# A recommender tower on one core: the last tile's second bias added on TensorE, its results stored as a column

## The reference

```
e = jnp.stack([tbl_0[ids[:, 0]], ..., tbl_31[ids[:, 31]]], axis=1)   # [2048, 32, 256]
dots = jnp.einsum('bnd,bmd->bnm', e, e)
z = dots[:, iu, ju]                                                  # i < j: 496 numbers
h = jnp.concatenate([z, dense_ctx], axis=1)                          # [2048, 512]
h = jnp.maximum(h @ W_top1 + b_top1, 0.0)                            # 512 -> 512
h = jnp.maximum(h @ W_top2 + b_top2, 0.0)                            # 512 -> 256
y = h @ W_top3                                                       # 256 -> 1
```

## Time and profile before

| | |
|---|---|
| median of 3 timed runs | 561.64 us (561.14 to 562.19) |
| the profiled execution: its own time | 563.57 us |
| its span, first to last instruction | 561.7 us |
| mean granted clock of TensorE | 0.988 of full speed |
| TensorE products, busy | 508.8 us, 91% of the span |
| VectorE, ScalarE, GpSimd busy | 45%, 33%, 71% |

### The profile page before, as it was taken

One profiled execution on the slowest core, in us unless ns is written; L12 is line 12 of the kernel. 1 busy time (PEld: TensorE's weight loads), 2 busy tenths in 40 slices (PEclk: granted clock), 3 DMA queues, 4 the chain that ended last, 5 costly groups with the idle time before them and its releaser, 6 DMA issues.

```text
span 561.7 us, 24241 instructions
## 1 busy us (share of the span) xinstructions
PE 508.8 (91%) x11019; PEld 467.3 (83%) x11019; DVE 250.8 (45%) x593; ACT 183.6 (33%) x354; POOL 397.6 (71%) x426
## 2 busy tenths in 40 slices
PE   0775799999899989999999999989998999989986
PEld 0765699999799979999989988979987899979885
DVE  3666362734336362343636263354626335351421
ACT  1786060513206051230505151140505114050422
POOL 6777577777777777777777777777777777777600
PEclk9997999999999999999999999999999999999998
DMA  8999344444444444444444444444444444433300
GB/s 190 272 261 305 116 117 125 118 120 116 124 121 125 118 116 118 121 125 116 124 121 120 124 113 119 121 125 117 117 128 113 122 116 118 116 107 106 97 2 1
DMA packets 37459, 70.97 MB, mean 126 GB/s; under 512 B 10382, under 2 KB 23438, under 8 KB 37358
## 3 DMA queue, kind: packets, MB, share of 16 engines
q0 software_dynamic: 20112, 54.95, 35.0%
q1 hardware_dynamic: 17246, 14.48, 10.4%
HBM read 69.39 MB, written 0.01 MB: 124 GB/s over the span
## 4 chain that ended last, share of the span: by engine, by line
PE 77%; DMA 7%; POOL 5%; issue 5%; ACT 3%; DVE 2%; DVEq 0%; ACTq 0%; POOLq 0%
PE look_ps L342 31%; PE quad_ps L364 16%; PE top_ps L415 10%; DMA rows<-in_tbl,row_ids 7%; PE turn_ps L326 6%; PE quad_ps L326 6%; POOL rows L299 5%; PE top_ps L428 5%; PE quad_ps L385 1%; PE top_ps L405 1%; DVE small L688 1%; DVE turned L626 1%; ACT area L526 1%; ACT products L520 0%; ACT turned L496 0%
## 5 line engine op out<-in xcount | busy, mean ns | idle before, releaser
L299 POOL DMA_INDIRECT rows<-in_tbl,row_ids x419 | 396.8, 947 | 132.1 <-issue 116.1
L342 PE MATMUL look_ps<-one_hot,small 125*128 125x256 f32 (+1 forms) x1536 | 221.0, 293 | 8.3 <-DVE small L688 8.0
L342 PEld LDWEIGHTS look_ps<-one_hot,small 125*128 125x128 f32 x1536 | 195.1, 192 | 11.9 <-issue 9.3
L698 DVE TENSOR_SCALAR one_hot<-ids_across,sub_row 125x256 fp32r<-125x256 int32 (+1 forms) x384 | 118.5, 380 | 121.0 <-PE look_ps L342 113.4
L364 PE MATMUL quad_ps<-turned 128*32 128x31 f32 x7680 | 103.5, 199 | 2.0 <-issue 1.5
L364 PEld LDWEIGHTS quad_ps<-turned 128*32 128x32 f32 x7680 | 85.8, 110 | 21.9 <-issue 2.6
L505 ACT ACTIVATE ahead<-look_ps 128x512 f32<-128x512 f32 (+1 forms) x48 | 28.0, 584 | 202.7 <-PE look_ps L342 202.5
L326 PE MATMUL turn_ps<-ident,rows 128*128 128x128 f32 x424 | 63.1, 280 | 22.3 <-DMA rows<-in_tbl,row_ids 20.7
L326 PE MATMUL quad_ps<-ident,rows 128*128 128x128 f32 x414 | 61.8, 280 | 13.2 <-DMA rows<-in_tbl,row_ids 10.3
L326 PEld LDWEIGHTS turn_ps<-ident,rows 128*128 128x128 f32 x424 | 47.4, 142 | 26.7 <-issue 15.5
L415 PE MATMUL top_ps<-area,w_sb 128*128 128x128 f32 x488 | 60.3, 283 | 1.0 <-ACT area L550 1.0
(11 more groups left out here) (51 smaller groups left out, 182.2 us busy)
## 6 DMA issues: line engine op xcount, KB each, us to landing
rows<-in_tbl,row_ids POOLq DMA_INDIRECT x419
ids_across<-in_small_ids SPq DMA_DIRECT2D x45, 128.0 KB
landed<-in_tbl SPq DMA_DIRECT2D x6, 896.0 KB
w_sb<-in_W_top SPq DMA_DIRECT2D x4, 256.0 KB
landed<-in_tbl SPq DMA_DIRECT2D x6, 104.0 KB
w_sb<-in_W_top SPq DMA_DIRECT2D x1, 512.0 KB
area<-in_dense_ctx SPq DMA_DIRECT2D x16, 8.0 KB, 1.9
row_ids<-in_ids SPq DMA_DIRECT2D x1, 240.0 KB, 13.2
```

What stands on the lines that cost most here:

```text
L299: pool.indirect_dma_start(out=rows[:, n % PLACES, j, :], out_offset=None, in_=tables[f], in_offset=bass.IndirectOffsetOnAxis(ap=row_ids[:, ...
L342: last = pe.matmul(look_ps[:, c * width:(c + 1) * width], small[:, f, r, part, c * P:(c + 1) * P], one_hot[n % 2][:, r, 0:width], start=(r ...
L698: last = dve.tensor_scalar(one_hot[n % 2][:, r, 0:width], ids_across[0:SP, n % IDS_RING, 0:width], sub_row[:, r:r + 1], None, ALU.is_equal)
```

## The change

For the last tile alone the second bias is no longer added by VectorE. TensorE opens the sum of layer 2 with a product of a row of ones (the first element of the identity, repeated 128 times) and the bias row, over a single partition; the four products of layer 2 then add to it. VectorE's one remaining instruction reads the sum as it stands. The results of the first 15 tiles are transposed and copied earlier, ahead of the last tile's tower, into `look_ps` and a `y_rows` of 15 rows, and stored by a transfer of their own; the second quarter of layer 1, which writes `look_ps`, waits for that copy. The last tile's 128 numbers go from their column of `y_sb` to DRAM, as 128 pieces of 4 bytes, by a second transfer that waits for `y_done`.

```
-        y_rows = area[0:TILES, 0:P]
+        y_rows = area[0:TILES - 1, 0:P]
...
             sp.wait_ge(y_kept, 1)
-            sp.dma_start(out.rearrange("(t p) a -> t (p a)", p=P), y_rows).then_inc(y_out, 16)
-            sp.wait_ge(y_out, 16)
+            sp.dma_start(out[0:BATCH - P, :].rearrange("(t p) a -> t (p a)", p=P), y_rows).then_inc(y_out, 16)
+            sp.wait_ge(y_done, TILES)
+            sp.dma_start(out[BATCH - P:BATCH, :], y_sb[:, TILES - 1:TILES]).then_inc(y_out, 16)
+            sp.wait_ge(y_out, 32)
...
-                                     w2_sb[:, c, :], start=(c == 0), stop=(c == M1 - 1))
+                                     w2_sb[:, c, :], start=(c == 0 and t < TILES - 1), stop=(c == M1 - 1))
                 last.then_inc(h2_done, 1)
+
+            def add_bias2():
+
+                pe.matmul(last_h2[:, 0:HIDDEN2], ident[0:1, 0:1].to_broadcast((1, P)), b2_sb[0:1, :],
+                          start=True, stop=False)
+
+            def turn_y():
+
+                pe.wait_ge(y_done, TILES - 1)
+                pe.transpose(look_ps[0:TILES - 1, 0:P], y_sb[:, 0:TILES - 1], ident[:, :]).then_inc(y_turned, 1)
...
+            turn_y()
             keep_running(2)
             turn_features(TILES - 1)
             for m in range(M1):
+                if m == 1:
+                    pe.wait_ge(y_kept, 1)
                 layer1(TILES - 1, m)
+            add_bias2()
             layer2(TILES - 1)
-
-            pe.wait_ge(y_done, TILES)
-            pe.transpose(top_ps[0:TILES, 0:P], y_sb[:, :], ident[:, :]).then_inc(y_turned, 1)
...
             keep_features(TILES - 1)
+            act.wait_ge(y_turned, 1)
+            act.activation(y_rows, look_ps[0:TILES - 1, 0:P], ACT.Copy).then_inc(y_kept, 1)
             keep_hidden1(TILES - 1)
-            act.wait_ge(y_turned, 1)
-            act.activation(y_rows, top_ps[0:TILES, 0:P], ACT.Copy).then_inc(y_kept, 1)
...
-                biased = bank[:, HIDDEN2:2 * HIDDEN2]
-                dve.tensor_tensor(biased, bank[:, 0:HIDDEN2], b2_sb[:, :], ALU.add).then_inc(h2_kept, 1)
-                dve.wait_ge(h2_kept, t + 1)
+                biased = bank[:, 0:HIDDEN2]
+                if t < TILES - 1:
+                    biased = bank[:, HIDDEN2:2 * HIDDEN2]
+                    dve.tensor_tensor(biased, bank[:, 0:HIDDEN2], b2_sb[:, :], ALU.add).then_inc(h2_kept, 1)
+                    dve.wait_ge(h2_kept, t + 1)
```

## The result

The changed kernel takes 570.32 us (median of 6 runs, 567.11 to 571.93) against 562.33 for the kernel before (6 runs, 561.14 to 565.64). The ratio on record is 1.0119, 95% interval 1.0091 to 1.0147: slower by 1.2%, some 6.7 us. The two medians lie 8.0 us apart, which is near the upper end of that interval. The forecast was no change.

The account below looks back on a forecast made before the run. TensorE, busy 91% of the span, bounds the body; the change touches only the uncovered end. The terms -0.47 + 0.44 - 0.62 + 0.3 = -0.35 us take 561.64 to 561.3 us, range 560.6 to 562.1.

Parts of the forecast that it names:

- The last store becomes a column: Final store: 128 pieces of one number instead of 16 rows, landing +0.1 to +0.5 us later, taken as +0.3.
- Rival 1: Column's store, issue to landing: each DMA engine's seven further pieces wait 0.35 us each, 2.45 more, 563.4 us; chance 0.07.
- The bias product: On TensorE between layer 1 and layer 2: two instructions of 0.2175 us, 0.44 in all, upper bound 0.76.
- no gap between products of unlike shape: From layer 1's products of 128 columns to layer 2's of 256 the chain shows no gap; reason for taking 0.44.
- no cover: Between layer 1 and layer 2 TensorE has no wait to hide the bias product, so it is paid in full.
- What left the end: End of kernel: the bias add leaves VectorE, -0.47 us; the transpose and copy no longer precede the store, -0.62.
- The moved work: Transpose (0.28 us) and copy (0.27) moved ahead of the last layers, hidden in idle time of TensorE and ScalarE.
- Rival 2: TensorE's clock, low from 551.2 to 554.6, stays up in most executions: 1.9 us saved, 559.4 us; chance 0.10.
- not 0.38: End of kernel: the span was said to end 0.38 us after the store's landing at 561.35.
- The 0.2% that a measurement was to tell: Timed result: a measurement can tell about 0.2% (1.12 us) from no change, so the likeliest verdict was no change.

Follow-up runs that it names:

- The probes: Changed kernel with extra stores ahead of its own, varying the pieces' spacing, number, size and sharing; single landings took 1.0 to 9.4 us.
- in the gap: Kernel before with the bias product directly behind the transposes of the last tile's features, where TensorE idles: 561.75 us against 562.5, ratio 0.9972.
- the probe by size: Changed kernel with extra stores of different piece sizes: 128 side by side landed in 7.2 and 8.5 us at 4 B, 1.4 at 64 B.
- the kernel with a single row: Changed kernel, bias product behind the features' transposes, last column turned, copied alone and stored as one 512 B row: 561.5 us against 561.88, ratio 1.0001.

## Why the prediction was wrong

**The step that failed** is "The last store becomes a column", with its bounds "+0.1 to +0.5" and the "+0.3" that went into the sum. It measured +6.8. I had priced it from the nearest row with 128 pieces, the load of `dense_ctx`. That row reads DRAM and has pieces of 64 B, which share no stretch of 32 B. The probes show that 128 pieces of 64 B, stored, do land in 1.4. So it was the right row for the number of pieces and the wrong one for what mattered, that 8 pieces share each 32 B.

**Rival 1** had the place, behind the issue of the column's store, and seven further pieces at a price each. But its seven were those of one DMA engine, and 128 pieces that lie 32 B apart cost nothing extra; the seven that count are those of the same 32 B. Its price of 0.35 came from the last packet's way to its landing; measured was 0.8. Its argument for, that the pieces lie next to each other, was the cause; its argument against was again the load's row. A chance of 0.07 was too little for a mechanism against which only a read stood. The changed kernel's column would be 1.4 and 7 x 0.8 = 5.6, together 7.0, and it landed in 8.2. The probes' values for 128 pieces side by side lie between 6.2 and 8.4, so single landings differ by over 1 us and the 0.8 is no more exact than that.

**The Trainium skill** ("DMA: Bandwidth & Descriptors", "Specifications") lets every piece under 512 B be a read-modify-write. These runs don't bear it out as a price by size: 128 pieces of 4 B, 32 B apart, landed in 1.4, as 16 rows of 512 B did. The rule pointed the right way, and that it came without a price was no ground to give it little weight.

**The bias product** was put at 0.44 with an upper bound of 0.76; it cost 0.81 with what it does to its neighbour. The reason given, no gap between products of unlike shape, held for columns and not for rows: all products in the earlier trace rows have 128 rows. The Trainium skill ("TensorE: Matmul & The Clock Gate", "Why this matters for your kernels") has a product over 32 partitions take as long as one over 128. No run here has 32; the one with a single row took 0.2 longer itself (0.62 against 0.43) and layer 2 behind it 0.2 more. That the product has no cover was right, and so was that the place decides: in the gap it is free.

**What left the end** was right. The add's 0.47 and the 0.62 of the transpose and the copy are the 1.10 measured. The moved work was hidden as said: the copy was done at 552.89, the second quarter's first weight load came at 553.70, the 15 rows landed in 1.3 at about 554.2.

**Rival 2, the clock.** It fell in the profiled execution after as it had before, and cost the same. The forecast had the price at 1.9; with layer 1's first two quarters at the full clock in the experiments (1.16 + 0.89 against 3.68) it is 1.63. All nine experiments have this stretch in their profile: seven ran it at the full clock, the one with a single row and the probe by size with the low one, so whether it falls differs. The moved transpose stands in four of the seven and in both of the two, so nothing here ties the fall to it. The argument that the three timed runs lay too close together for a mixture rested on three runs only: 25 later ones of the kernel before lie between 560.98 and 566.46, further apart than a fall costs. The chain of the kernel with a single row:

```profile
552.69 2.02 PE top_ps L418 x8
554.71 1.66 PE look_ps L418 x8
```

**A small slip.** The span ends 561.7 - 561.35 = 0.35 behind the landing, not 0.38; no term rests on it. The 0.2% that a measurement was to tell was too hopeful: with ten runs of an experiment the intervals reach about 0.3% to each side.

**What stays open.** Sharing alone does not give the time in every case: 16 pieces side by side, one from each of 16 partitions, share a stretch by eights too and took 2.3 to 2.4, 32 took 4.4 to 5.0, where 64 took 6.4 to 7.2 and 127 even 8.3 to 9.4. Why few are cheaper and 127 dearer is not settled, nor what in the memory's path waits. All stores went to the same output, so whether other places or queues pay the same is untested. Nor is it known why a product of one row disturbs the next.

## What to carry to other kernels

Don't end a kernel with a store of many single numbers that lie side by side in DRAM: turn them into rows first, even at 0.6 us, since pieces that share each 32 B by eights made the landing some 6 us longer here. When an operation has no row in the trace, ask of the nearest row not only how many pieces it has but whether it reads or writes and what its pieces share; if they differ in that, its value bounds nothing. A small product put among big ones is best placed where TensorE waits anyway: there it cost nothing, on the path it cost more than the add that it replaced.

## What the runs showed of the hardware

- Stores of 4 B pieces: 1.4 us from issue to landing with 128 of them 32 B apart; about 0.8 us more for each further piece within the same 32 B with 8 (7.0) or 4 (3.8), from the same partition or from others. With 2 it was 1.3 to 2.5. Exceptions: 16 and 32 pieces side by side, with 2.3 to 2.4 and 4.4 to 5.0.
- The DMA engines' packets of the changed kernel's column were all done within 1.2 us of its issue; the wait is behind them and is in no engine's busy time.
- A store of one row of 512 B took 1.0 us, of 16 such rows 1.4, of 4 rows of 128 B 1.7.
- An fp32 product of 256 columns over one partition between products over 128: 0.62 us and 0.20 more for the next eight instructions; over 128 partitions 0.43 and nothing.
